# Two window-attention blocks on one core: a new order on the step grid, X loaded image by image, constant rows written by ScalarE

## The chip, the cores and the metric

The kernel runs on one core of a Trainium2 chip. The metric is the device time of one execution in microseconds (us), lower is better; 2% is about what the runs of this kernel can tell from no change. TensorE, VectorE (DVE), ScalarE (ACT), GpSimd (POOL) and SyncE (SP) each work through their own list of instructions in order and wait on semaphores.

## The reference

Two transformer blocks in a row, each on 8 images of 16x16 tokens with 192 channels, in fp32:

```
xn   = layer_norm(x) * w + b
win  = 14x14 windows of xn padded to 28x28          # 4 windows an image, 196 tokens each
q,k,v = win @ qkv_w + qkv_b                         # 12 heads of 16
attn = softmax(q*scale @ k.T + rel_h(q) + rel_w(q)) # over all 196 keys, padded ones too
x    = x + (attn @ v) @ proj_w + proj_b
x    = x + gelu(layer_norm(x)*w+b @ fc1_w + fc1_b) @ fc2_w + fc2_b
```

The second block has its own weights and a different epsilon.

## The kernel before

The 8 images go through layer 0 and then through layer 1, as a pipeline of 16 "images" n = 0 to 15 (layer L = n // 8). X stays in SBUF for all images. An image's tokens are ordered so that the first 224 are the window's columns and the last 32 the edge.

For one image the steps are: the statistics and the normalised `xhat` of the first norm (`stats1`, GpSimd's `root1`, `hat1`), transposes and a split in a high and a low fp32r part (`norm1`, `low1`), the products `q`, `k`, `v`, the relative-position products `rel0` and `rel1` (28 small matmul rows each) and their transposes `rel_tok`. All of these use one PSUM bank, `front`. GpSimd makes the low parts of q, k and rel; SP copies them row group by row group into `q_stack` and `k_stack` (`qk0`, `rel0`, `stack1`: 20 DMAs an image), so that one product of 108 rows gives a head's scores. Then come, for each of 12 heads, `by_query` (scores with the queries in partitions) and `row_max`; `top` joins the maxima; `neg_top` transposes them and SP adds them as two rows to `q_stack`; `by_key` gives the scores again, transposed and with the maximum taken off, and ScalarE's `probs` exponentiates them. `times_v` (three groups of four heads), `to_tokens`, `att`, `proj`, the second norm (`stats2`, `root2`, `hat2`, `norm2`, `low2`), `fc1` (three pairs), ScalarE's `gelu` and `fc2` end the image. The padded keys are worked out apart, on GpSimd and VectorE (`pad_...`). ScalarE changes its function table between exponentials and gelus.

The order on each engine is written out by hand as a grid. Each engine has a table of ticks (`PE_AT`, `ACT_AT`, `DVE_AT`, `POOL_AT`, `SP_AT`), and `run` emits a step of image n at tick 48 n + its own:

```python
for now in range(min(ticks), PERIOD * (2 * IMAGES - 1) + max(ticks) + 1):
    for step in steps:
        for n in range(2 * IMAGES):
            if now - PERIOD * n in ticks:
                step(n, n // IMAGES, n % 2, now - PERIOD * n)
```

So ticks give an order and no time. The steps of up to four images stand between each other. The bank `back1` (`BB[1]`) is shared by `neg_top`, `proj` and two pairs of fc1; `issued` and `neg_tops_out` write the waits that follow from the order.

All loads stand in SP's one list. In the kernel before it begins with image 0's X, `ident`, vectors, qkv weights and masks; then the constant rows of both stacks (a mask and one-hot rows, rounded by GpSimd's `round_rows` to `rows_rounded` and copied 12 times by four DMAs); between them the rest of X in one DMA; then projection and fc2 weights and biases of both layers, then fc1's weights of layer 0 (`load_w1`) into the buffer that qkv's weights leave, and only then the grid, with `qk0` of image 0 first. The weights are split in high and low parts by ScalarE and VectorE (`weights1`, `weights2`), and norm biases go through the weights as small products (`bias0`, `bias1` for qkv, `bias2` for fc1).

## Time and profile before

| | us |
|---|---|
| runs (3) | 671.58, 660.64, 670.36; median 670.36 |
| the profiled execution | 666.7 |
| its span, first to last instruction | 664.8 |
| TensorE busy | 558.1 (84%) |
| VectorE, ScalarE, GpSimd busy | 361.0, 305.5, 236.1 |
| mean granted TensorE clock | 0.902 |

Times in rows are us from the span's start. "[x <-A]" behind a row is the engine's idle time before it and what ended it. A granted clock of 1.00 is 2.4 GHz and 0.50 is 1.2 GHz; the records begin some 80 us into the span, and before that the rows' own durations tell the level. A busy TensorE isn't TensorE at its peak.

### The profile page before, as it was taken

Reading aid. Unit: us, or ns where it says so; the run is one execution under the profiler, and the core shown is the slowest. Engines: PE = TensorE matmul, PEld = TensorE weight load, DVE = VectorE, ACT = ScalarE, POOL = GpSimd, SP = SyncE. Lnnn points to the kernel's source line nnn. Section 1 sums busy time; section 2 is a strip of 40 time slices with the busy share of each in tenths; the row PEclk is TensorE's granted clock in tenths of the full one; section 3 lists DMA queues with packets and bytes.
Section 4 is the critical chain, followed back from the end, with each engine's and each line's share of the span. In section 5 each row is a group of like instructions: output and inputs, shape, how many; then the busy total and the mean of one; then the engine's idle time right before and its main releaser. Section 6 shows DMA issues by size and latency. Waiting matters only on the chain.

```text
span 664.8 us, 12602 instructions
## 1 busy us (share of the span) xinstructions
PE 558.1 (84%) x4440; PEld 502.5 (76%) x4440; DVE 361.0 (54%) x914; ACT 305.5 (46%) x614; POOL 236.1 (36%) x424
## 2 busy tenths in 40 slices
PE   5700778989898989899998989898989998978766
PEld 4700667779797979798897978797979887967646
DVE  3210265685848484856448575758584767473221
ACT  1100113347463736464344737474745574746522
POOL 2001354253625343441515252354444263430100
PEclk9999977599989898997689988999897999999777
DMA  4416523322222222224112222222231323220000
GB/s 99 107 47 172 107 52 70 85 68 69 52 54 58 58 59 58 59 58 101 42 37 45 61 55 58 59 57 61 57 72 43 86 53 76 57 71 27 1 12 13
DMA packets 45674, 41.10 MB, mean 62 GB/s; under 512 B 6268, under 2 KB 44588, under 8 KB 45612
## 3 DMA queue, kind: packets, MB, share of 16 engines
q1 hardware_dynamic: 45612, 40.29, 25.9%
q8 instruction: 36, 0.59, 0.4%
q14 instruction: 26, 0.21, 0.1%
HBM read 6.80 MB, written 1.57 MB: 13 GB/s over the span
## 4 chain that ended last, share of the span: by engine, by line
PE 55%; issue 13%; DVE 9%; SPq 9%; POOL 8%; ACT 3%; DMA 3%; POOLq 0%; DVEq 0%; ACTq 0%
PE front L917 11%; PE back L831 10%; PE back L1073 9%; PE by_key L940 5%; PE by_query L971 5%; PE front L831 4%; DVE xhat L671 3%; SPq L297 3%; PE times_v L957 2%; POOL norm_rstd L394 2%; SPq L293 2%; POOL pad_e L423 2%; SPq L289 2%; PE back L1053 1%; DVE att L750 1%
## 5 line engine op out<-in xcount | busy, mean ns | idle before, releaser
L768 DVE TENSOR_REDUCE row_max<-by_query 128x2 f32<-128x512 f32 x192 | 130.7, 682 | 48.9 <-PE by_query L971 47.7
L530 ACT ACTIVATE probs<-by_key 128x452 f32<-128x452 f32 x192 | 103.5, 543 | 84.9 <-PE by_key L940 84.3
L940 PE MATMUL by_key<-q_stack,k_stack 110*128 110x196 f32 (+1 forms) x384 | 89.7, 331 | 2.2 <-ACT probs L530 1.9
L971 PE MATMUL by_query<-k_stack,q_stack 108*128 108x256 f32 x384 | 84.8, 314 | 8.0 <-DMA q_stack<-rel_lo 7.7
L917 PEld LDWEIGHTS front<-q_grid,rel_heads 96*84 96x84 f32 x896 | 86.9, 181 | 3.8 <-ACT rel_t L556 1.9
L917 PE MATMUL front<-q_grid,rel_heads 96*84 96x32 f32 (+1 forms) x896 | 87.7, 265 | 2.2 <-ACT rel_t L556 1.4
L940 PEld LDWEIGHTS by_key<-q_stack,k_stack 110*128 110x128 f32 x384 | 63.9, 210 | 14.7 <-issue 7.3
L971 PEld LDWEIGHTS by_query<-k_stack,q_stack 108*128 108x128 f32 x384 | 65.5, 213 | 10.0 <-DMA q_stack<-rel_lo 9.5
L1073 PE MATMUL back<-w,hid 128*128 128x192 f32 x384 | 70.9, 337 | 0.4 <-ACT hid L595 0.3
L1073 PEld LDWEIGHTS back<-w,hid 128*128 128x128 f32 x384 | 65.0, 198 | 1.2 <-ACT hid L595 0.8
L831 PE MATMUL back<-xn_hi,w_hi 128*128 128x256 f32 x192 | 61.3, 328 | 2.7 <-DVE xn_hi L678 2.7
L831 PE MATMUL back<-xn_hi,w_lo 128*128 128x256 f32 x192 | 60.3, 323 | 0.0
L394 POOL TENSOR_TENSOR norm_rstd<-norm_var,minus_half 128x2 f32<-128x2 f32 x32 | 30.0, 939 | 75.4 <-DVE norm_var L663 74.1
L671 DVE TENSOR_TENSOR xhat<-xhat,norm_rstd 128x384 f32<-128x384 f32 x32 | 32.0, 1001 | 42.9 <-POOL norm_rstd L394 42.9
L715 DVE COPY rel_t<-front 84x448 f32<-84x448 f32 x16 | 9.9, 621 | 82.0 <-PE front L917 82.0
L448 POOL TENSOR_TENSOR pad_w<-pad_w,pad_prod 128x36 f32<-128x36 f32 x16 | 4.2, 263 | 138.5 <-ACT pad_w L570 138.5
L831 PEld LDWEIGHTS back<-xn_hi,w_hi 128*128 128x128 f32 x192 | 45.7, 238 | 3.6 <-DVE xn_hi L678 3.6
L957 PE MATMUL times_v<-probs,v_ones 128*32 128x256 f32 (+1 forms) x768 | 48.2, 370 | 0.0
L831 PEld LDWEIGHTS back<-xn_hi,w_lo 128*128 128x128 f32 x192 | 45.2, 236 | 0.0
L488 POOL CAST rel_hi<-rel_t 84x512 fp32r<-84x512 f32 x32 | 19.5, 609 | 71.9 <-DVE rel_t L716 59.0
L595 ACT ACTIVATE hid<-back,b_real 128x256 f32<-128x256 f32 x96 | 38.8, 473 | 10.6 <-PE back L831 10.4
L490 POOL TENSOR_TENSOR rel_lo<-rel_t,rel_hi 84x512 fp32r<-84x512 f32 x32 | 40.8, 1276 | 2.6
(142 smaller groups left out, 1102.7 us busy)
## 6 DMA issues: line engine op xcount, KB each, us to landing
q_stack<-q_hi SPq DMA_DIRECT2D x64, 96.0 KB
k_stack<-k_hi SPq DMA_DIRECT2D x64, 96.0 KB
q_stack<-rel_hi SPq DMA_DIRECT2D x64, 84.0 KB
q_stack<-rel_lo SPq DMA_DIRECT2D x64, 84.0 KB
q_stack<-q_lo SPq DMA_DIRECT2D x32, 96.0 KB
k_stack<-k_lo SPq DMA_DIRECT2D x32, 96.0 KB
out<-X SPq DMA_DIRECT2D x8, 192.0 KB, 2.2
k_stack<-xn_hi SPq DMA_DIRECT2D x2, 744.0 KB
```

Of the source, the lines that this page charges most:

```text
L394: pool.tensor_tensor(norm_rstd[i][:, :], norm_var[i][:, :], minus_half[:, :], ALU.pow).then_inc(n_rstd[i], 1)
L490: pool.tensor_tensor(rel_lo[par][:, w, :, :], rel_t[:, w, :, :], rel_hi[par][:, w, :, :].bitcast(F32), ALU.subtract).then_inc(s_rlo, 1)
L530: act.activation(probs[h % NP][:, :], KB[h % 2][:, 0:KEYS], ACT.Exp).then_inc(s_ex, 1)
L595: act.activation(hid[:, m, :], fc1_psum(m), ACT.Gelu, bias=b1_real[L][:, m:m + 1]).then_inc(s_ge, 1)
L671: dve.tensor_tensor(xhat[i][:, :, :], xhat[i][:, :, :], norm_rstd[i][:, :].unsqueeze(2).broadcast_to([P, TILES, D]), ALU.mult).then_inc(n_ ...
L768: dve.tensor_reduce(row_max[:, h, :], QB[h % 2][:, :].rearrange("p (a t) -> p a t", a=TILES), AX, ALU.max).then_inc(s_smax, 1)
L831: last = pe.matmul(psum, lhs, rhs, start=(i == 0), stop=(i == len(chunks) - 1))
L917: last = pe.matmul(dst[:, :, at, :], rel_heads[L][:, w, WS - 1 - i:2 * WS - 1 - i, :] .rearrange("p k h -> p (k h)"), grid[:, :, at, :], s ...
L940: last = pe.matmul(KB[h % 2][:, lo:hi], k_stack[par][0:ROWS, h, c * P:(c + 1) * P], q_stack[par][0:ROWS, h, 0:hi - lo], start=True, stop=True)
L957: last = pe.matmul(VB[i * VW:(i + 1) * VW, 0:hi - lo], v_ones[n % NV][:, c, h, :], probs[h % NP][:, lo:hi], start=(c == 1), stop=(c == 0))
L971: last = pe.matmul(QB[h % 2][:, a * TOK:(a + 1) * TOK], q_stack[par][0:R_MAX, h, a * P:(a + 1) * P], k_stack[par][0:R_MAX, h, :], start=Tr ...
L1073: last = pe.matmul(BB[0][:, a * D:(a + 1) * D], hid[:, m, a * P:(a + 1) * P], w2[L][:, m, :], start=(m == 0), stop=(m == MC - 1))
```

## The change

- X is loaded image by image, each into its own semaphore, in SP's grid (`x` at the very start).
- The constant rows of both stacks are written by ScalarE (`stack_constants`: four copies of a whole stack from `key_rows` and `query_rows`), two at the start of its list and two after image 0's `q_grid`. GpSimd's `round_rows` and the four DMAs go, and so do the waits of `norm2` and `by_query` for them; SP's first `qk0` of each stack waits instead.
- The late weights of a layer (`load_late`) are asked for in SP's grid, layer 0's after image 1's stacks and layer 1's after image 3's; `proj_b` of layer 0 comes earlier. Each layer has its own semaphores. `load_w1` of layer 0 stands in the grid before image 0's `qk0`, qkv's weights of layer 1 one image later.
- fc1's bias product (`bias2`) is made before image 2's (10's) norm1 in place of image 1's (9's).
- Nearly all ticks of all five tables are new. On TensorE image 0's list begins bias0, norm1, q, k, v, rel0, rel1, rel_tok, then norm1, q, k, v of image 1, then by_query of image 0; before, bias2 and norm1 of image 1 and by_query of image 0 came ahead of q of image 1. On VectorE `setup` and `bias0` now come first. On ScalarE no `probs` stands between an image's three gelu steps. On GpSimd `fc2_bias` follows `root2` at once. The outputs are all stored after the last image's rows.

```diff
@@ -40,7 +40,7 @@
 V_LOADS = 16 * 2 * 2
-W_LOADS = 16 * 2 * 5
+W_LOADS = 16 * 3
 EPS = (1e-5, 1e-6)
...
@@ -48,20 +48,20 @@
 
-PE_AT = dict(bias0=-42, bias1=-51, bias2=-48, norm1=-47, q=-41, k=-35, v=-30, rel0=-21, rel1=-15, rel_tok=-11,
-             by_query=(5, 6, 10, 14, 18, 22, 25, 29, 31, 34, 39, 42), neg_top=52,
-             by_key=(56, 60, 62, 65, 72, 76, 77, 81, 83, 87, 92, 96), times_v=(74, 87, 104), to_tokens=106, att=110,
-             proj=114, norm2=123, fc1=(127, 128, 132), fc2=(140, 148))
-ACT_AT = dict(weights1=-45, weights2=40, norm1=-46, q_hi=-35, q_grid=-36, k_hi=-27, rel0=-14, rel_tok=-1, pad_e=26, pad_w=63,
-              att=116, neg_top=51, probs=(62, 64, 68, 74, 76, 78, 82, 86, 90, 95, 99, 103), norm2=124,
-              gelu=(132, 135, 137))
-DVE_AT = dict(stats1=-58, hat1=-52, low1=-47, weights1=-45, weights2=47, bias0=-43, bias1=-50, bias2=-49, setup=-31, q=-42, k=-32, v=-23,
-              rel1=-17, pad_max=15, pad_sum=27, pad_top=34,
-              row_max=(5, 9, 13, 15, 19, 25, 27, 28, 32, 37, 40, 43), top=45, times_v=(78, 88, 105), att=108,
-              x_att=116, stats2=120, hat2=120, low2=123, x_mlp=149)
-POOL_AT = dict(norm_b=-45, root1=-46, proj_bias=-32, pad_shift=23, pad_join=30, pad_arg=59, pad_mul=59, pad_sum=66,
-               pad_out=78, fc2_bias=128, root2=121, q_lo=-21, k_lo=-22, rel0=-6, rel1=-4)
-SP_AT = dict(qk0=-10, rel0=2, stack1=37, neg_top=66, wqkv=7, w1=-19, out=213)
+PE_AT = dict(bias0=-399, bias1=-54, bias2=-53, norm1=-47, q=-43, k=-42, v=-39, rel0=-30, rel1=-18, rel_tok=-11,
+             by_query=(17, 18, 24, 28, 29, 36, 37, 39, 40, 50, 51, 52), neg_top=54,
+             by_key=(57, 61, 62, 64, 68, 69, 73, 74, 79, 81, 85, 86), times_v=(72, 82, 102), to_tokens=109, att=119,
+             proj=121, norm2=131, fc1=(136, 144, 147), fc2=(149, 150))
+ACT_AT = dict(constants=(-384, -48), weights1=-79, weights2=39, norm1=-62, q_hi=-46, q_grid=-50, k_hi=-40, rel0=-30,
+              rel_tok=-20, pad_e=10, pad_w=67, att=107, neg_top=41,
+              probs=(46, 47, 53, 57, 58, 64, 66, 69, 70, 74, 85, 91), norm2=122, gelu=(126, 129, 132))
+DVE_AT = dict(stats1=-83, hat1=-70, low1=-45, weights1=-50, weights2=78, bias0=-338, bias1=-47, bias2=-51,
+              setup=-368, q=-36, k=-30, v=-22, rel1=-10, pad_max=23, pad_sum=27, pad_top=48,
+              row_max=(26, 28, 32, 35, 36, 38, 39, 48, 49, 50, 53, 55), top=55, times_v=(82, 92, 121), att=122,
+              x_att=129, stats2=130, hat2=130, low2=136, x_mlp=165)
+POOL_AT = dict(norm_b=-332, root1=-56, proj_bias=135, pad_shift=56, pad_join=67, pad_arg=77, pad_mul=115,
+               pad_sum=122, pad_out=137, fc2_bias=161, root2=161, q_lo=13, k_lo=13, rel0=21, rel1=27)
+SP_AT = dict(x=-803, late=-16, qk0=-96, rel0=-94, stack1=-72, neg_top=-45, wqkv=-97, w1=-98, out=348)
 
...
@@ -182,12 +181,13 @@
 
-        s_x0, s_x, s_const = sem("x0_loaded"), sem("x_loaded"), sem("const_loaded")
-        s_vec, s_w, s_wx, s_wy = sem("vectors_loaded"), sem("weights_loaded"), sem("wqkv_loaded"), sem("w1_loaded")
+        s_x, s_const = [sem(f"x{n}_loaded") for n in range(IMAGES)], sem("const_loaded")
+        s_vec, s_wx, s_wy = sem("vectors_loaded"), sem("wqkv_loaded"), sem("w1_loaded")
+        s_pb, s_b2, s_w = ([sem(f"{x}{L}_loaded") for L in range(2)] for x in ("proj_b", "fc2_b", "back_weights"))
         s_zero, s_wz = sem("buffers_zeroed"), sem("proj_weights_zeroed")
-        s_eps, s_rows, s_rounded = sem("eps_ready"), sem("stack_rows_loaded"), sem("stack_rows_rounded")
+        s_eps, s_rows = sem("eps_ready"), sem("stack_rows_loaded")
         s_id, s_col = sem("ident_loaded"), [sem(f"columns_loaded{L}") for L in range(2)]
-        s_setup, s_stack0 = sem("vectors_ready"), [sem(f"stack{i}_constants_loaded") for i in range(2)]
+        s_setup, s_stack0 = sem("vectors_ready"), sem("stack_constants_ready")
         s_nb, s_wxh, s_wxl = sem("norm_bias_widened"), sem("wqkv_hi_done"), sem("wqkv_lo_done")
...
@@ -270,39 +270,36 @@
 
-            sp.dma_start(x_slot(0, 0), x_t[:, 0:TILES, :]).then_inc(s_x0, 16)
-            sp.dma_start(ident[:, :], const["ident"]).then_inc(s_id, 16)
-            sp.dma_start(columns[0][:, :], layers[0]["columns"]).then_inc(s_col[0], 16)
-            load_wqkv(0)
-            sp.dma_start(columns[1][:, :], layers[1]["columns"]).then_inc(s_col[1], 16)
+            sp.dma_start(x_slot(0, 0), x_t[:, 0:TILES, :]).then_inc(s_x[0], 16)
             sp.dma_start(key_rows, const["key_rows"]).then_inc(s_rows, 16)
             sp.dma_start(query_rows, const["query_rows"]).then_inc(s_rows, 16)
+            sp.dma_start(columns[0][:, :], layers[0]["columns"]).then_inc(s_col[0], 16)
+            sp.dma_start(ident[:, :], const["ident"]).then_inc(s_id, 16)
+            load_wqkv(0)
+            sp.dma_start(pb[0][:, :], layers[0]["proj_b"].unsqueeze(0).broadcast_to([P, D])).then_inc(s_pb[0], 16)
             for name, tile in (("pad_mask", pad_mask[:, :, :]), ("head_mask", head_mask[:, :])):
                 sp.dma_start(tile, const[name]).then_inc(s_const, 16)
+            sp.dma_start(columns[1][:, :], layers[1]["columns"]).then_inc(s_col[1], 16)
             for L in range(2):
...
                 sp.dma_start(rel[L][:, :, :], p["rel"]).then_inc(s_vec, 16)
-            for par in range(2):
-                sp.wait_ge(s_rounded, 1)
-                for stack, lo, hi, c in ((q_stack, R_MASK, R_MAX, 1), (k_stack, R_RHI, ROWS, 0)):
-                    sp.dma_start(stack[par][lo:hi, :, :].bitcast(F32),
-                                 rows_rounded[lo:hi, c:c + 1, :].bitcast(F32).broadcast_to([hi - lo, HEADS, TOK])
-                                 ).then_inc(s_stack0[par], 16)
-                if par == 0:
-                    sp.dma_start(X[:, TILES:, :], x_t[:, TILES:, :]).then_inc(s_x, 16)
-            for L in range(2):
+
+            def load_late(L):
                 p = layers[L]
-                for tile, name in ((pb[L], "proj_b"), (b2[L], "fc2_b")):
-                    sp.dma_start(tile[:, :], p[name].unsqueeze(0).broadcast_to([P, D])).then_inc(s_w, 16)
+                if L == 1:
+                    sp.dma_start(pb[1][:, :], p["proj_b"].unsqueeze(0).broadcast_to([P, D])).then_inc(s_pb[1], 16)
+                sp.dma_start(b2[L][:, :], p["fc2_b"].unsqueeze(0).broadcast_to([P, D])).then_inc(s_b2[L], 16)
                 sp.wait_ge(s_wz, L + 1)
-                sp.dma_start(wp[L][:, 0, :], p["proj_w"][0:P, :]).then_inc(s_w, 16)
-                sp.dma_start(wp[L][0:LO, 1, :], p["proj_w"][P:D, :]).then_inc(s_w, 16)
-                sp.dma_start(w2[L][:, :, :], p["fc2_w"].rearrange("(m f) n -> f m n", f=P)).then_inc(s_w, 16)
-            sp.wait_ge(s_wxl, 1)
-            sp.wait_ge(s_wxh, 2)
-            sp.wait_ge(s_bx, 1)
-            load_w1(0)
+                sp.dma_start(wp[L][:, 0, :], p["proj_w"][0:P, :]).then_inc(s_w[L], 16)
+                sp.dma_start(wp[L][0:LO, 1, :], p["proj_w"][P:D, :]).then_inc(s_w[L], 16)
+                sp.dma_start(w2[L][:, :, :], p["fc2_w"].rearrange("(m f) n -> f m n", f=P)).then_inc(s_w[L], 16)
+
+            def setup(n, L, par, t):
+                if t == SP_AT["x"] and 1 <= n < IMAGES:
+                    sp.dma_start(x_slot(0, n), x_t[:, n * TILES:(n + 1) * TILES, :]).then_inc(s_x[n], 16)
+                if t == SP_AT["late"] and n in (0, 2):
+                    load_late(n // 2)
 
...
@@ -331,6 +328,8 @@
                 if t == SP_AT["qk0"]:
+                    if n < 2:
+                        sp.wait_ge(s_stack0, 2 * (n + 1))
                     load_qk_rows(n, par, 0)
...
@@ -346,22 +345,22 @@
             def store(n, L, par, t):
-                if t == SP_AT["wqkv"] and n == 2:
+                if t == SP_AT["wqkv"] and n == 3:
                     sp.wait_ge(s_wyl, 1)
...
                     load_wqkv(1)
-                if t == SP_AT["w1"] and n == IMAGES:
-                    sp.wait_ge(s_wxl, 2)
-                    sp.wait_ge(s_wxh, 4)
-                    sp.wait_ge(s_bx, 2)
-                    load_w1(1)
+                if t == SP_AT["w1"] and n % IMAGES == 0:
+                    sp.wait_ge(s_wxl, L + 1)
+                    sp.wait_ge(s_wxh, 2 * (L + 1))
+                    sp.wait_ge(s_bx, L + 1)
+                    load_w1(L)
                 if t == SP_AT["out"] and L == 1:
...
 
-            run(SP_AT, stack_neg_top, load_stacks, store)
+            run(SP_AT, setup, stack_neg_top, load_stacks, store)
             sp.wait_ge(s_out, 16 * IMAGES)
...
@@ -399,19 +394,16 @@
 
-            def widen_norm_b():
-                for L in range(2):
-                    pool.wait_ge(s_col[L], 16)
-                    pool.tensor_copy(norm_b[L][:, :, :],
-                                     n1[L][:, :, 1:2].broadcast_to([P, 2, P])).then_inc(s_nb, 1)
+            def widen_norm_b(L):
+                pool.wait_ge(s_col[L], 16)
+                pool.tensor_copy(norm_b[L][:, :, :], n1[L][:, :, 1:2].broadcast_to([P, 2, P])).then_inc(s_nb, 1)
 
             def biases_and_pads(n, L, par, t):
-                if t == POOL_AT["norm_b"] and n == 0:
-                    round_rows()
-                    widen_norm_b()
+                if t == POOL_AT["norm_b"] and n in (0, 1):
+                    widen_norm_b(n)
                 if t == POOL_AT["proj_bias"]:
                     pool.wait_ge(n_hat[0], n + 1)
-                    pool.wait_ge(s_w, W_LOADS)
+                    pool.wait_ge(s_pb[L], 16)
                     add_bias(L, n, pb[L], s_xb)
...
@@ -500,7 +493,15 @@
 
+            def stack_constants(par):
+                act.wait_ge(s_rows, 32)
+                for stack, rows in ((k_stack, key_rows), (q_stack, query_rows)):
+                    act.activation(stack[par][:, :, :], rows.unsqueeze(1).broadcast_to([P, HEADS, TOK]),
+                                   ACT.Copy).then_inc(s_stack0, 1)
+
             def weights(n, L, par, t):
+                if t in ACT_AT["constants"] and n == 0:
+                    stack_constants(ACT_AT["constants"].index(t))
                 if t == ACT_AT["weights1"] and n % IMAGES == 0:
...
@@ -515,9 +516,6 @@
                 act.wait_ge(s_vp if i == 0 else s_f1, n if i == 0 else MC * n)
-                if i == 1 and n == 0:
-                    for par in range(2):
-                        act.wait_ge(s_stack0[par], 32)
                 act.activation(xn_hi[i][:, 0, :], bank[:, 0:TOK], ACT.Copy)
...
@@ -618,7 +616,7 @@
                     scaled_lo(w1_lo, w1_in, n2[L], w1_hi, MLP, L, s_wyh, s_wyl)
-                if t == DVE_AT["bias2"] and n % IMAGES == 1:
+                if t == DVE_AT["bias2"] and n % IMAGES == 2:
                     dve.wait_ge(s_by, L + 1)
...
@@ -800,10 +798,8 @@
                 if t == DVE_AT["stats1"]:
-                    if n == 0:
-                        dve.wait_ge(s_x0, 16)
-                    else:
-                        dve.wait_ge(s_x, 16)
+                    if L == 0:
+                        dve.wait_ge(s_x[n], 16)
                     if L == 1:
...
@@ -963,8 +959,6 @@
                         pe.wait_ge(*stack_loaded(n, h // GH))
-                    if h == 0 and n < 2:
-                        pe.wait_ge(s_stack0[n], 32)
                     if HEADS * n + h >= 2:
...
@@ -1027,12 +1021,12 @@
                         pe.wait_ge(s_bxo, L + 1)
-                    if n % IMAGES == 1:
+                    if n % IMAGES == 2:
                         pe.wait_ge(s_byo, L + 1)
...
                     pe.wait_ge(s_ato, n + 1)
-                    pe.wait_ge(s_w, W_LOADS)
+                    pe.wait_ge(s_w[L], W_LOADS)
                     pe.wait_ge(s_zero, ZEROED)
```

## Rows read from the trace of the kernel before

**Rows 1.** The page, part 2: TensorE, busy tenths of the span in 40 slices.

```profile
PE   5700778989898989899998989898989998978766
```

**Rows 2.** Waits of TensorE, 0 to 99 us: line and releaser; us, times, longest.

```profile
PE front L844 <- DMA weights_in<-in_fc_w: 30.8, 1, 30.8
...
PE by_query L971 <- DMA q_stack<-rel_lo: 3.4, 1, 3.4
```

**Rows 3.** Timeline of SP's issues, 0 to 66 us: start, us, what.

```profile
10.15 14.94 SPq L293 DMA_DIRECT2D X<-in_x  x1
...
34.31 15.12 SPq L297 DMA_DIRECT2D pb<-in_proj_b  x1
```

**Rows 4.** Windows: length, each engine busy (instructions), granted clock, DMA share, GB/s.

```profile
159.84:578.43 418.59, 390.83 (x3308) 356.97 (x3307) 266.43 (x674) 228.13 (x460) 174.42 (x299) 0.92 0.26 59
194.50:229.14 34.64, 32.38 (x274) 29.82 (x273) 21.99 (x57) 18.77 (x39) 14.60 (x25) 0.90 0.26 56
295.42:338.15 42.73, 40.66 (x294) 36.61 (x293) 24.00 (x62) 20.12 (x41) 14.61 (x25) 0.80 0.28 64
515.60:547.18 31.58, 29.56 (x274) 26.78 (x273) 22.00 (x57) 18.79 (x39) 14.63 (x25) 1.00 0.30 68
603.57:664.80 61.23, 43.69 (x268) 37.17 (x266) 14.38 (x42) 23.48 (x42) 5.67 (x9) 0.77 0.04 14
```

**Rows 5.** Timeline of VectorE: the `top` of images 0 and 2.

```profile
99.03 0.18 DVE L792 TENSOR_TENSOR top<-row_max,pad_top 128x24 f32<-128x24 f32 x1
...
159.84 0.18 DVE L792 TENSOR_TENSOR top<-row_max,pad_top 128x24 f32<-128x24 f32 x1
```

**Rows 6.** Waits of TensorE, 515.6 to 547.18 us.

```profile
PE back L837 <- DVE xhat L671: 1.2, 1, 1.2
PE back L1053 <- DVE av_t L776: 0.3, 1, 0.3
PE by_query L971 <- DMA q_stack<-rel_lo: 0.3, 1, 0.3
```

**Rows 7.** Windows of 5 us beside the fall of the clock.

```profile
210.00:215.00 5.00, 3.24 (x41) 2.89 (x30) 4.49 (x8) 0.65 (x2) 4.90 (x11) 0.88 0.00 0
215.00:220.00 5.00, 5.00 (x26) 5.00 (x26) 1.02 (x2) 3.15 (x6) 3.10 (x4) 0.50 0.30 79
```

**Rows 8.** Timeline of all engines, 0 to 35 us: the front of image 0.

```profile
3.28 0.62 DVE L653 BATCH_NORM_STATS2 norm_s<-X 128x6 f32<-128x192 f32 x2 [3.28 <-DMA X<-in_x]
...
7.27 0.38 ACT L521 ACTIVATE xn_hi<-front 128x256 fp32r<-128x256 f32 x1 [5.18 <-PE front L839]
...
7.89 0.43 SPq L285 DMA_DIRECT2D att<-in_rel  x1
...
8.39 0.42 DVE L678 TENSOR_TENSOR xn_hi<-front,xn_hi 64x256 fp32r<-64x256 f32 x1
...
14.02 0.53 PE L831 MATMUL front<-xn_hi,wqkv_hi 128*96 128x256 f32 x1
...
21.27 0.49 DVE L644 TENSOR_TENSOR rel_heads<-att,head_mask 96x324 f32<-96x324 f32 x1
```

**Rows 9.** DMA issues of the whole run: queue, count, size, median us to landing.

```profile
att<-in_rel SPq DMA_DIRECT2D x2, 20.2 KB, 3.1
```

**Rows 10.** Groups by line and form, 121 to 590 us: busy us, mean ns, idle before.

```profile
L595 ACT ACT_TABLE_LOAD x26 | 33.4, 1283 | 0.5
...
L574 ACT ACTIVATE hid<-back 128x512 f32<-128x512 f32 x14 | 8.4, 598 | 23.4 <-PE back L1063 23.4
```

**Rows 11.** Timelines of VectorE and GpSimd, 520 to 552 us: second norm, `k_lo`, first norm.

```profile
528.73 0.56 DVE L814 TENSOR_TENSOR X<-X,back 128x384 f32<-128x384 f32 x1
...
531.49 1.61 DVE L671 TENSOR_TENSOR xhat<-xhat,norm_rstd 128x384 f32<-128x384 f32 x1 [0.59 <-POOL norm_rstd L394]
...
531.42 1.26 POOL L483 TENSOR_TENSOR k_lo<-k_t,k_hi 96x512 fp32r<-96x512 f32 x1
...
546.72 0.55 DVE L671 TENSOR_TENSOR xhat<-xhat,norm_rstd 128x384 f32<-128x384 f32 x1
```

7 lines of the change are left out of this document (2 added, 5 removed).

## The prediction, made before the changed kernel ran

> **What bounds the kernel now.** I read the page's slices first. TensorE is nearly full in the middle, and thin at both ends [rows 1]. TensorE's list of waits up to 99 us names the hole at the start: 30.8 us for fc1's weights, then 3.4 us for the last stack rows [rows 2]. The weights come late because SP's list stands in order behind 14.94 us of issuing the rest of X and 15.12 us of the next load [rows 3], with four copies of constant rows between. So one list of transfers sets the start.
>
> The stretches from one `top` to another come next [rows 4, 5]. From image 2's to image 14's are 418.6 us, 34.9 an image. One image at full clock took 31.58 us with TensorE busy for 29.56; the waits that ended there add up to 2.0 us (three are shown, the fourth is 0.2), 1.2 of them for the second norm's `hat2` [rows 4, 6]. TensorE is the bound with little idle, so a new order can take out at most these 2 us of a full-clock image. But the other image shown took 34.64 us with the same 274 matmul rows, at a granted clock of 0.90 [rows 4]. In detail: a stretch with 3.24 us of work in 5 is followed by five at 0.50, the 1.2 GHz level [rows 7]. So the hole costs twice where the clock falls: some 3.1 us more (34.64 - 31.58).
>
> **The start.** Five things change; the sum is for image 0's `top`, at 99.03 us now [rows 5].
> (a) The 30.8 us go: fc1's weights are asked for behind seven X loads and the first projection's end, and their bias product stands one image later, behind image 0's by_query steps. What is late next is the front chain of image 0. (b) The 3.4 us go: SP has nothing between image 0's rows and their wait. (c) Against it, VectorE's first step is now `setup`, which waits for the last small load. That load was issued at 7.89 us and is one place further back now; with the 3.1 us that its kind took to land it ends near 11.5. Two set-up pairs to 21.76 from 20.71 are 1.05 us (the last row of these shown), the bias sum 0.4. From the statistics' start (3.28) to `low1`'s end (8.81) are 5.5 us. So the first q product starts at 11.5 + 1.4 + 5.5 + 0.6 of hand-overs = 19.0, not 14.02: +5 us [rows 8, 9]. (d) ScalarE writes the constant rows: four copies of 128x3072. Nothing like it is in the trace; a 128x512 one took 0.598 [rows 10]. Bounds: 0.6 each if only the fixed part counted, 3.6 by length in proportion; I take 2.8, from the slope between 128x256 (0.38) and 128x512 [rows 8, 10]. The first two (5.6 us from about 4.6) end near 10.2, under the wait of (c), then the hi weights follow; the second two stand between `q_grid` and `q_hi`, where only SP's stack loads wait, and those are due 20 us later. Cost 0; if the cover failed, 0 to 7 us each pair. In return SP loses four copies of up to 744 KB. (e) q, k and v of image 1 now all stand ahead of image 0's first by_query: about +1 us net, as they were needed anyway.
> Sum: -30.8 - 3.4 + 5 + 1 = -28 us, `top` of image 0 at 71 (66 to 76).
> X in seven pieces costs seven issues of about 0.4 to 0.6 us in place of 14.94 [rows 3], beside VectorE's wait. The Trainium skill speaks against it ("DMA: Bandwidth & Descriptors", section Bandwidth: transfers should be batched to a MiB or more to get three quarters of the peak). By that rule the seven would take longer in total than the one of 1344 KB; the row shows the one held up by its queue for 14.94 us, and image 1 needs only its own piece, so the sum stays as it is.
>
> **The first two full images.** From image 0's `top` to image 2's are 60.8 us now [rows 5], much of it at the low level. The back half is not yet there, so they are bound by the chain, with fewer holes in the new order: I take 56, between 60.8 (nothing) and 50. That is -5.
>
> **The steady part.** I walked one image through the new order with starts and durations of the full-clock image. On TensorE it is now: norm1, two by_query, fc1's third pair, q, fc2, neg_top, k, fc2, times_v, v, two by_key, to_tokens, ..., att, by_query, times_v, proj, two by_key, two by_query, rel1, two by_key, times_v, norm2. Between proj's end and norm2 lie four score steps (0.24 us each), rel1 (2.2), two more and a times_v (0.9): 4.5 us. VectorE and GpSimd need 2.76 us from x_att's start to `hat2`'s (528.73 to 531.49) and then `hat2` itself: 3.4 us. It took 1.61 us beside GpSimd's `k_lo`, and 0.55 alone [rows 11]. In the new order GpSimd waits for `hat2` right after the root (`fc2_bias`), so nothing runs beside it. The 1.2 us wait goes, with 1.1 to spare; to_tokens and att also get 1 us and more of cover. What is late next is `low1` before q and `low2` before fc1, which come through ScalarE behind gelus: 0.2 to 0.4 us each. GpSimd's list (14.6 us busy an image [rows 4]) and SP's keep their cyclic order; neg_top's rows land 1.3 us before by_key asks.
> ScalarE's exponentials no longer stand between the gelus: two table loads of 1.283 us an image in place of four (two groups of 26 in 13 images, one of them shown [rows 10]). ScalarE isn't the bound, so 2.6 us saved count as cover only.
> So an image takes 29.6 + 0.6 = 30.2 us, bounds 29.6 and 31.6. Twelve are 362; the layer change adds bias products and weight splits, as now (42.73 us for the image with it [rows 4]): 9. That is 371 against 418.6: -47. It takes for granted that the clock stays at 2.4 GHz: no stretch as thin as the one before the fall is left, since both rel steps now stand among dense score steps.
> A rule against this is in the Trainium skill ("SBUF — State Buffer", Who interferes with whom: a VectorE instruction with both inputs in SBUF and a GpSimd one that reads SBUF shut each other out). The 1.61 beside 0.55 us agrees. By it `hat1`, which now falls beside `k_lo`, takes 1.1 us more; VectorE is busy 22 of 31.6 us there and `hat1` is due 10 us later, so it changes nothing unless VectorE becomes the bound.
>
> **The end.** The last `top` to the end are 61.2 us, TensorE busy 43.7 [rows 4]: a serial chain of the last two images. Its order is almost the same; fewer table loads give -1.5 (0 to -4).
> **Sum** for the profiled execution (666.7 us; span 664.8 and 1.9 around it): -28 - 5 - 47 - 1.5 = -81.5, so 585. The median of the runs is 670.4, so some 588; I say 587.
>
> **The rivals.**
> R1, the clock falls as often as now. For: it fell in the start inside rel steps with hardly a hole before them, and in the new order rel1, times_v and norm2 stand nearly together. Against: the clean falls follow the norm2 hole. Price 3.07 us (34.64 - 31.58) in some 9 of 12 images: +27, 613.
> R2, the steady part gains nothing, because a wait of the same size takes the place of `hat2`'s (my slacks are about 1 us, over 100 steps with four lists in order). Only the start is won: 670 - 34 = 636 (626 to 652).
> R3, the start isn't won, since `setup` and the constant rows hold the front longer: (d) uncovered for both pairs, +11, and the start's own slow clock, +3: 601. It lies in the range.
> R4, slower: TensorE stays at the low level through much of the steady part, because four mid-size waits keep it thin in place of one. An image of 29.6 us of work at half the granted rate costs up to 50. The start's gain of 34 over 14 images is 2.4 us each, so it decides from 34.9 + 2.4 = 37.3 us an image, a low share of over a third in place of 0.16 of the time (clock 0.92 [rows 4]). The start of before had such a share. It would give 690.
> That the change doesn't do what it says can't be: the loads are in the lists as written; R3 is what comes nearest.
>
> **How the numbers follow.** Forecast (570 to 602) 0.60; R1 0.17; R3 0.06; R2 0.12; R4 0.03; better than my bounds 0.02. The low end: start 66, images of 29.6, end -4, gives 566. Range 566 to 622: it leaves out R2, R4 and the tails, some 0.2. Within 2% (about what this kernel's runs can tell from none, 657 to 684) lies only the worst of R2: 0.03. Slower 0.03, faster 0.94.
>
> **What would show it.** First q product near 19 us; no wait over 7 us on TensorE after it; image 0's `top` near 71 and image 2's near 127; 30.2 us from one `top` to the next; the wait before norm2 gone; 2 table loads an image; a mean granted clock of 0.95 or more in the middle. The forecast is wrong if TensorE shows new waits of over 1 us in each image, above all before q, fc1's first pair or by_key, or if the clock falls in each image all the same.

## The result and the profile after

The changed kernel takes 570.7 us (median of four runs, 569.7 to 571.6). The kernel before took 668.2 us beside it (660.6 to 671.6). The ratio is 0.857, 95% interval 0.849 to 0.865. Some executions are in a slower state at a lower clock, and the ratios and their intervals leave those out (here the one of 671.6 us), while the medians don't, so the medians of the kernel before come out 2 to 5 us too high. The profiled execution's span is 568.8 us against 664.8.

The page's second part comes first again; it answers to [rows 1]. The second line is the granted clock of the same slices in tenths.

```profile
PE   3587989999999999999999999999999999989856
...
PEclk9999579999999999979998999999999999999987
```

TensorE is 90% busy or more from the seventh slice to the thirty-fifth. The clock falls at 59 us, in the slices with 243 and 308 us, and in the last images.

The windows of the changed kernel, cut at the `top` of images 2 and 14, 5 and 6, 6 and 7, and 15 and the end, answer to [rows 4]: length, then busy us of TensorE, its weight loads, VectorE, ScalarE and GpSimd, granted clock, DMA share, GB/s.

```profile
128.39:493.61 365.22, 362.84 (x3301) 330.66 (x3301) 271.23 (x671) 196.40 (x435) 170.38 (x299) 0.98 0.30 68
187.32:216.77 29.45, 29.25 (x274) 26.64 (x274) 22.51 (x56) 16.20 (x37) 14.20 (x25) 1.00 0.30 66
216.77:251.89 35.12, 34.92 (x293) 31.46 (x291) 24.81 (x60) 17.08 (x39) 15.13 (x25) 0.90 0.24 60
517.17:568.80 51.63, 37.43 (x262) 31.67 (x260) 14.00 (x42) 19.90 (x38) 7.65 (x12) 0.90 0.10 32
```

The twelve images of the first line took 418.59 us before, with TensorE busy for 390.83. So idle time went from 27.8 to 2.4 us (-25.4) and busy time from 390.8 to 362.8 us (-28.0) on nearly the same instructions (3308 and 3301). The second part is the clock: the same products at the high level are shorter. The gain in the middle is thus one half holes and one half clock.

The list of TensorE's waits in one steady image (187.32 to 216.77 us) has one row left. It answers to [rows 6], where three rows made up 1.8 us.

```profile
PE back L827 <- DVE xn_hi L676: 0.2, 1, 0.2
```

Where the 96.0 us of span went, between the `top` rows of VectorE at 77.97, 128.39, 493.61 and 517.17 us:

| stretch | before | after | forecast | measured |
|---|---|---|---|---|
| start to image 0's `top` | 99.0 | 78.0 | -28 | -21.1 |
| to image 2's `top` | 60.8 | 50.4 | -5 | -10.4 |
| to image 14's `top` | 418.6 | 365.2 | -47 | -53.4 |
| to image 15's `top` | 25.1 | 23.6 | (0) | -1.6 |
| to the end | 61.2 | 51.6 | -1.5 | -9.6 |

The start fell short, and these rows of its timeline say where; they answer to [rows 8]. The first is VectorE's `setup`, waiting for the last small load; the second is the first q product; the last three are image 1's second relative product, the first pair of fc1's bias product, and the transposes of the norm that come after it.

```profile
14.10 0.17 DVE L636 SCALAR_TENSOR_TENSOR kb_blocks<-head_mask,columns 96x12 f32<-96x12 f32 x1 [14.10 <-DMA att<-in_rel]
...
20.98 0.53 PE L827 MATMUL front<-xn_hi,wqkv_hi 128*96 128x256 f32 x1 [1.62 <-DVE xn_hi L676]
...
59.75 4.04 PE L913 MATMUL front<-q_grid,rel_heads 96*84 96x64 f32 x28
...
67.03 0.49 PE L840 MATMUL front<-columns,weights_in 128*128 128x1 f32 x2
...
73.61 0.66 PE L833 MATMUL front<-ident,xhat 128*128 128x128 f32 x2 [0.46 <-DVE b_real L621]
```

The q product stands at 20.98 and not at 19.0. The small load was issued at 8.36 us and landed 5.7 us later, not 3.1 [rows 9]; most of the delay has another cause, though, which the section on the prediction shows. And the relative product of 28 instructions takes 4.04 us, the time of the low level (2.2 at the high one), and fc1's bias product 6.1 us (67.03 to about 73.1). While it runs VectorE waits 7.43 us, and the last by_query steps of image 0 come behind it. So it lies on the path to image 0's `top`, as experiment 7 confirms.

### The profile page after: what moved, and what is told of

It is laid out like the page before. It is cut to its first block, busy times and chain, and to the rows that moved or that the text cites. A ratio compares the mean times of both kernels' runs of the same rounds, so it can differ in the third digit from the quotient of the medians.

```text
span 568.8 us, 12594 instructions
## 1 busy us (share of the span) xinstructions
PE 522.0 (92%) x4440; PEld 468.5 (82%) x4440; DVE 367.0 (65%) x914; ACT 277.3 (49%) x588; POOL 230.9 (41%) x423
## 4 chain that ended last, share of the span: by engine, by line
PE 68%; issue 14%; DVE 8%; POOL 5%; SPq 1%; ACT 1%; DMA 1%; DVEq 0%; POOLq 0%; ACTq 0%
PE back L827 12%; PE front L827 12%; PE front L913 11%; PE back L1067 9%; PE by_query L965 5%; PE times_v L953 5%; PE by_key L936 5%; DVE row_max L766 4%; DVE xn_hi L676 1%; POOL norm_rstd L389 1%; PE front L841 1%; PE front L840 1%; DMA att<-in_rel 1%; POOL X L394 1%; PE front L833 1%
## 5 line engine op out<-in xcount | busy, mean ns | idle before, releaser
L913 PE MATMUL front<-q_grid,rel_heads 96*84 96x32 f32 (+1 forms) x896 | 78.8, 252 | 1.4 <-ACT rel_t L554 0.7
L913 PEld LDWEIGHTS front<-q_grid,rel_heads 96*84 96x84 f32 x896 | 78.5, 166 | 1.9 <-DVE v_ones L703 0.9
L965 PE MATMUL by_query<-k_stack,q_stack 108*128 108x256 f32 x384 | 72.8, 305 | 1.6 <-DVE row_max L766 1.3
L936 PE MATMUL by_key<-q_stack,k_stack 110*128 110x196 f32 (+1 forms) x384 | 71.9, 304 | 2.2 <-DMA q_stack<-neg_top_t 1.1
L965 PEld LDWEIGHTS by_query<-k_stack,q_stack 108*128 108x128 f32 x384 | 56.6, 200 | 4.2 <-DVE row_max L766 3.3
L936 PEld LDWEIGHTS by_key<-q_stack,k_stack 110*128 110x128 f32 x384 | 53.3, 190 | 6.9 <-ACT probs L528 2.4
L827 PE MATMUL back<-xn_hi,w_lo 128*128 128x256 f32 x192 | 53.9, 293 | 0.0
L827 PE MATMUL front<-xn_hi,wqkv_hi 128*96 128x256 f32 x128 | 39.7, 320 | 6.5 <-DVE xn_hi L676 3.5
L827 PE MATMUL front<-xn_hi,wqkv_lo 128*96 128x256 f32 x128 | 37.1, 300 | 0.0
L953 PEld LDWEIGHTS times_v<-probs,v_ones 128*32 128x32 f32 x768 | 20.1, 109 | 17.8 <-issue 3.7
L472 POOL TENSOR_TENSOR q_lo<-q_t,q_hi 96x512 fp32r<-96x512 f32 x16 | 20.5, 1283 | 33.0 <-ACT q_hi L537 33.0
```

The costliest lines, as they stand in the source:

```text
L472: pool.tensor_tensor(q_lo[par][:, :, :], q_t[:, :, :], q_hi[par][:, :, :].bitcast(F32), ALU.subtract).then_inc(s_qlo, 1)
L827: last = pe.matmul(psum, lhs, rhs, start=(i == 0), stop=(i == len(chunks) - 1))
L913: last = pe.matmul(dst[:, :, at, :], rel_heads[L][:, w, WS - 1 - i:2 * WS - 1 - i, :] .rearrange("p k h -> p (k h)"), grid[:, :, at, :], s ...
L936: last = pe.matmul(KB[h % 2][:, lo:hi], k_stack[par][0:ROWS, h, c * P:(c + 1) * P], q_stack[par][0:ROWS, h, 0:hi - lo], start=True, stop=True)
L953: last = pe.matmul(VB[i * VW:(i + 1) * VW, 0:hi - lo], v_ones[n % NV][:, c, h, :], probs[h % NP][:, lo:hi], start=(c == 1), stop=(c == 0))
L965: last = pe.matmul(QB[h % 2][:, a * TOK:(a + 1) * TOK], q_stack[par][0:R_MAX, h, a * P:(a + 1) * P], k_stack[par][0:R_MAX, h, :], start=Tr ...
```

## The experiments

In each the theory called A is that of the prediction, or of my explanation of its miss. Unless another is named, each kernel is the changed one with the edit shown.

**1 and 2. The two parts apart.** The first has the new loads and constant rows with the old grid, the second the old loads with the new grid. The first cut is against the kernel before; ScalarE's table there also has the two steps of the constant rows, which the cut leaves out, and fc1's bias product is the late one.

```diff
 e1: PE_AT, ACT_AT, DVE_AT, POOL_AT as before
-SP_AT = dict(qk0=-10, rel0=2, stack1=37, neg_top=66, wqkv=7, w1=-19, out=213)
+SP_AT = dict(x=-803, late=-16, qk0=-96, rel0=-94, stack1=-72, neg_top=-45, wqkv=-97, w1=-98, out=348)
 e2: build() as before; all grids as after, without x, late and constants, and
+wqkv=-49
```

> The changed kernel's loads, constant rows and late bias product of fc1, in the grid of before (PE, ACT, DVE and POOL tables of before, with the two constant steps at the start of ScalarE's list and after q_grid). Theory A, start and order are two separate gains: the 30.8 us wait for fc1's weights and the 3.4 us for the stack rows go and nothing else, so 668 - 34 = 634 us (626 to 642), the wait of norm2 on hat2 stays at 1.2 to 1.8 us in each image, and the mean clock stays near 0.90. Rival B, the start is won only together with the order (another wait of the old grid ends late in its place): over 650. Rival C, the loads alone also mend the steady part: under 615.

> The loads, the rounded constant rows and the early bias product of before, in the new grid. Theory A: the hole of 30 us on TensorE before 66 us stays, images come every 29.5 us in the middle at full clock, and the end takes about 52 us in place of 61; the sum is the changed kernel's 571 plus 28 to 34, so 602 (595 to 610). Rival B, the order needs the new loads to run (SP's list blocks it later too): over 625. Rival C, the order is worth less than the trace of the changed kernel suggests, since the early start only moves the phase at which the clock falls: 620 to 635 with falls in most images.

Measured: the new loads alone 630.9 us, ratio 0.958 (0.947 to 0.969); the new grid alone 598.2 us, ratio 0.910 (0.904 to 0.916), against 662.1 for the kernel before on the same chip. In ratios that is 0.042 and 0.090 off, together 0.132, where both at once took off 0.143. Each of the three has an interval of about 0.01 to either side, so the parts add up as closely as these runs can tell. Both times lie where they were expected.

With the new loads alone image 0's `top` stands at 64.85 us, 34.2 sooner than before, the whole of terms (a) and (b) (in it 0.9 us are an earlier first q product, 13.07 for 14.02). With the new grid alone it stands at 105.28, 6.2 later, the size of (c) and (e) together, though other waits lie there as well. The middle remains as it was: the waits of TensorE between the `top` of images 2 and 14 still hold `hat2`'s, and the window is nearly that of before.

```profile
PE back L833 <- DVE xhat L669: 21.1, 12, 1.8
...
129.47:542.20 412.73, 384.02 (x3308) 351.40 (x3307) 266.41 (x674) 228.19 (x460) 174.09 (x299) 0.93 0.26 61
```

With the new grid alone the middle is that of the changed kernel, and a little better:

```profile
157.40:519.70 362.30, 359.99 (x3301) 328.22 (x3301) 271.24 (x670) 196.42 (x435) 170.02 (x299) 0.99 0.29 66
```

So the middle belongs to the grid and the start to the loads.

**3, 4 and 10. Give the hole back.** If the wait for `hat2` is what brought the clock down, putting the second norm's transposes six steps sooner, with all else left, should bring both back. The rival is that a hole costs only its own length. In the third kernel rel1 stands behind the hole; in the fourth it was to stand ahead of it; in the tenth it stands behind times_v.

```diff
-             proj=121, norm2=131
+             proj=121, norm2=125          # all three
-rel1=-18, rel_tok=-11
+rel1=-24, rel_tok=-11                     # the fourth
+rel1=-13, rel_tok=-9                      # the tenth, and VectorE's rel1=-9
```

> The changed kernel with TensorE's norm2 moved ahead of rel1, so that only four score steps lie between proj and norm2: a wait for hat2 of some 2.4 us in each image, straight before the rel products. Theory A, a hole ahead of rel products makes the clock fall: an image takes 29.5 + 2.4 at full clock and 3 us more where the clock falls, in most images, so 571 + 14 x 2.4 = 605 without falls and 625 to 640 with them; mean clock 0.93 or less. Rival B, the falls came from elsewhere (the phase, or the start): 605, clock 0.96.

> As the run before it, with rel1 moved ahead of proj, so that the same hole before norm2 is followed by by_key and times_v steps and not by rel products. Theory A, it is the hole and the thin rel products together that bring the clock down: the hole of 2 to 2.4 us stays, but few or no falls, 600 to 610 us, clock 0.95 or more. Rival B, the hole alone does it: the same time and clock as the run with the rel products behind it, within 1%.

> The transposes of the second norm stand 6 steps sooner on TensorE, and the second relative product and its copies behind times_v, so that by_key and times_v stand behind the hole instead of the relative products. Theory A (a short hole in each image costs mostly through the clock, wherever it stands): hat2's wait is 1.2 to 2.6 us an image, the clock falls in most images, an image costs 34 to 38 us instead of 29.46, and the total is 640 to 680. Theory B (only a hole that thin relative products follow brings the clock down): an image costs 29.46 plus the hole, 31 to 32 us, the clock stays above 0.95 and the total is 590 to 605.

Measured: 676.7, 715.3 and 668.6 us; the ratios are 1.029 (1.023 to 1.037), 1.090 (1.080 to 1.101) and 1.007 (1.002 to 1.013). One step moved by six places of the order undoes the whole gain of 14%. The first two expectations were well too low under every theory they named; the tenth kernel's theory A (640 to 680 us, a wait of 1.2 to 2.6 us, a fall in most images) came true. Waits and windows of TensorE from image 2's to image 14's `top`, of the third kernel:

```profile
PE back L833 <- DVE xhat L669: 30.7, 12, 2.8
...
137.70:596.00 458.30, 427.52 (x3301) 387.45 (x3301) 272.69 (x671) 195.32 (x435) 168.99 (x299) 0.82 0.24 55
```

and of the tenth:

```profile
PE back L833 <- DVE xhat L669: 30.8, 12, 2.8
...
140.60:584.60 444.00, 410.98 (x3301) 368.35 (x3301) 270.65 (x670) 194.93 (x435) 169.29 (x299) 0.87 0.24 56
```

The hole is 2.6 us an image in both (30.7 and 30.8 over 12). The third kernel's middle is 93.1 us longer than the changed kernel's, 28.4 of it idle (458.3 - 427.5 against 2.4) and 64.7 of it the same 3301 instructions at a lower clock. In the tenth it is 78.8 us, 30.6 idle and 48.1 clock. The fourth was no clean test: rel1 now comes so soon behind rel0 that it waits for ScalarE's copy of rel0's result out of the bank they share (`rel_t`, 18.4 us in 12 images), besides `hat2` (28.6 us). Its middle has 47.5 us idle and 443.8 busy, so it shows only that a second hole costs more of the same.

Three windows of the tenth kernel around one hole (197.59, 2.54 us of waiting) answer to [rows 7]:

```profile
190.00:195.00 5.00, 5.00 (x49) 4.21 (x47) 3.70 (x8) 2.75 (x8) 0.80 (x1) 1.00 0.35 96
195.00:200.00 5.00, 2.46 (x25) 1.55 (x24) 3.32 (x10) 1.99 (x6) 3.23 (x9) 0.84 0.24 41
200.00:205.00 5.00, 5.00 (x39) 4.61 (x32) 0.00 (x0) 0.00 (x0) 2.71 (x6) 0.50 0.00 0
```

The rival's condition, that only a hole with the relative products behind it brings the clock down, fell. In the tenth kernel transposes, two by_key and a times_v stand behind the hole, and the clock is at its low level in the window from 199 us, before the relative product begins:

```profile
198.00:199.00 1.00, 1.00 (x10) 0.71 (x12) 0.64 (x2) 0.51 (x2) 0.83 (x3) 0.70 0.00 0
199.00:200.00 1.00, 1.00 (x16) 0.40 (x8) 0.00 (x0) 1.00 (x4) 0.98 (x6) 0.50 0.00 0
...
200.40 4.13 PE L913 MATMUL front<-q_grid,rel_heads 96*84 96x64 f32 x28
```

In both kernels the clock falls beside each of the twelve holes. The falls last longer in the third, so the place has a share of it, 64.7 against 48.1 us.

**5 and 11. The exponential between the gelus.** In the changed kernel the twelve exponentials no longer part the three gelus. The fifth kernel puts the one of head 10 back, between the second gelu and the third, ahead of the copy of the next image's norm; the eleventh behind that copy.

```diff
-probs=(46, 47, 53, 57, 58, 64, 66, 69, 70, 74, 85, 91)
+probs=(46, 47, 53, 57, 58, 64, 66, 69, 70, 74, 82, 91)    # the fifth
+probs=(46, 47, 53, 57, 58, 64, 66, 69, 70, 74, 83, 91)    # the eleventh
```

> The softmax exponential of head 10 is put back between the first and the second gelu, so ScalarE changes its table four times an image instead of twice: two more loads of 1.28 us, and the second gelu ends about 3 us later. Theory A (the two fewer table loads are cover only, as the prediction had it): the second gelu is late for fc2 by 0 to 2 us; the steady images cost 29.5 to 31 us instead of 29.46, and the total is 571 to 592. Theory B (ScalarE's saving is a real part of the gain): the wait of fc2 on the second gelu is over 2 us in each image, the clock falls beside it as in the kernel before, and the total is above 600.

> The exponential of head 10 stands between the two gelus again, with its two table loads, but behind the copy of the next image's norm instead of ahead of it. Theory A (the run with the split ahead of that copy lost its 1.9 us an image because q waited for that copy; the table loads themselves are cover): q waits no longer, the second gelu ends 3 us later and fc2 waits 0 to 1 us, an image costs 29.5 to 30.5 us, and the total is 571 to 583. Theory B (two more table loads and the exponential cost an image about as much wherever they stand): fc2 waits for the second gelu by 1.5 to 3 us, an image costs 31 to 32.5 us, and the total is 590 to 610.

Measured: 600.3 us (597.8 to 604.0) and 579.1 us (577.9 to 581.2), ratios 0.911 (0.906 to 0.917) and 0.873 (0.869 to 0.877). The fifth's time lies at the edge of its theory B (over 600) and above A, but neither mechanism is the one that ran: fc2 doesn't wait for the gelus in the middle. The eleventh bears out its theory A. ScalarE's timeline of the fifth shows why:

```profile
189.28 1.28 ACT L528 ACT_TABLE_LOAD   x1
190.58 0.55 ACT L528 ACTIVATE probs<-by_key 128x452 f32<-128x452 f32 x1
191.02 0.38 ACT L519 ACTIVATE xn_hi<-front 128x256 fp32r<-128x256 f32 x1
...
191.67 1.28 ACT L593 ACT_TABLE_LOAD   x1
```

The copy of the next image's norm stands behind the table load and the exponential, VectorE's low part behind the copy, and q behind that. TensorE's wait for it is 19.0 us in eleven images, at most 1.9:

```profile
PE front L827 <- DVE xn_hi L676: 19.0, 11, 1.9
...
129.60:516.30 386.70, 365.49 (x3302) 333.31 (x3301) 271.35 (x672) 227.06 (x455) 170.41 (x299) 0.98 0.28 64
```

In the eleventh, q doesn't wait, and an ordinary image takes 29.8 us in place of 29.46. So two more table loads cost 0.35 us an image in the middle. In the last stretch they cost more: 57.0 us from image 15's `top` in the eleventh kernel, 60.8 in the fifth, 51.6 in the changed one, 61.2 before. fc2 waits there for the gelus:

```profile
PE back L1067 <- ACT hid L593: 3.4, 2, 2.1
```

The fifth kernel holds a second finding. Its hole before q, 1.7 us an image, is as long as the one that the kernel before had at the second norm in the same images:

```profile
PE back L837 <- DVE xhat L671: 19.1, 12, 1.8
```

Yet its middle has only 2.7 us more of busy time than the changed kernel's, where the kernel before had 28. The fifth kernel's window with one such hole (1.87 us) kept the full clock:

```profile
190.00:195.00 5.00, 3.13 (x25) 2.92 (x24) 3.14 (x9) 3.77 (x7) 0.84 (x2) 1.00 0.26 69
```

TensorE did less in these 5 us than in the stretch before the fall in [rows 7] (3.13 against 3.24). But the hole didn't leave the clock alone throughout. Of the nine holes of 1.9 us in the fifth kernel's middle, those that end at 159.7, 290.3 and 453.5 us are followed by a fall:

```profile
161.00:164.00 3.00, 3.00 (x12) 3.00 (x11) 2.77 (x11) 0.00 (x0) 1.67 (x3) 0.52 0.00 0
291.00:294.00 3.00, 3.00 (x13) 3.00 (x12) 2.71 (x10) 0.52 (x2) 1.22 (x2) 0.50 0.11 29
455.00:458.00 3.00, 3.00 (x11) 3.00 (x11) 2.61 (x10) 0.00 (x0) 1.87 (x3) 0.50 0.00 0
```

Each lasts 3.4 us. In the kernel before a fall of 3.4 to 10.2 us follows seven of the nine holes of 1.8 us in its middle. So a hole of nearly the same length brought the clock down in most images in one kernel and in a third of them in the other, and neither its length nor the busy share of 5 us tells by itself whether it will. What stands beside the hole differs: fc1 ahead and q and fc2 behind in the fifth, by_query and times_v ahead and the relative product behind in the kernel before. No run changed that alone with a hole of this length, so why the one costs more clock than the other stays open.

**6, 7 and 8. The start's two delays.** The sixth kernel takes VectorE's bias and setup out of the way of the first q product; the seventh moves fc1's bias product one image later; the eighth does both.

```diff
-bias0=-338, ... setup=-368
+bias0=-44, ... setup=-29                      # sixth, eighth
-if t == PE_AT["bias2"] and n % IMAGES == 2:   # and so on VectorE, and in norm1's wait
+if t == PE_AT["bias2"] and n % IMAGES == 3:   # seventh, eighth
-if t == SP_AT["wqkv"] and n == 3:
+if t == SP_AT["wqkv"] and n == 4:             # seventh, eighth
```

> VectorE's bias of q,k,v and its setup stand right ahead of the copy of q for image 0 and no longer ahead of the splits of the first weights. Theory A (the 2 us by which q.0 came later than forecast, 20.98 instead of 19.0, are the late landing of the small load, 5.7 us after its issue instead of 3.1): the first q product stands near 16 to 17, image 0's top near 73 to 74, and the time is 4 us less, 566 to 568. Theory B (the weight splits or the low parts of the image are as late anyway): q.0 stays at 20 to 21 and the time stays within 1 us of 570.7.

> The product of the second norm's bias through fc1 (12 pairs of narrow products) is moved one image later, and the next layer's q,k,v load with it. Theory A (it stood in image 0's path at the low clock, 6.1 us, and would take 3 us at the high one): image 0's top comes 6 us sooner, near 72, 3 us come back later, and the time is 3 us less, 567 to 569. Theory B (VectorE or the stack rows of image 0 hold its top anyway): image 0's top stays at 77 to 78 and the time stays within 1 us of 570.7, or rises by 3 us.

> The two edits before this one together. If both delays stand on the one chain to image 0's top, the gains add: 7 to 8 us, 562 to 565. If one hides the other, the total is that of the better of the two, 566 to 568.

Measured on one chip: 565.7 us (563.9 to 576.7), 569.2 (567.0 to 572.4) and 566.1 (562.8 to 572.1); ratios 0.859 (0.854 to 0.864), 0.864 (0.860 to 0.868), 0.858 (0.853 to 0.864). The first q product of the sixth comes at the expected place:

```profile
16.09 0.53 PE L827 MATMUL front<-xn_hi,wqkv_hi 128*96 128x256 f32 x1 [1.62 <-DVE xn_hi L676]
```

Image 0's `top` comes to 75.2 (73 to 74 expected), 72.7 and 68.5 us, from 78.0. So both delays lie on its path and they add (2.8 + 5.3 = 8.1, measured 9.5; the five other kernels with this start and X in seven pieces have that `top` at 77.3 to 79.3, so a difference of 1 us tells nothing). The total doesn't follow: the eighth is no faster than the sixth, where 562 to 565 were expected if the gains added. In the seventh, the step from image 0's `top` to image 1's takes 30.0 us in place of 23.0, and in the eighth 27.6: the bias product and the low clock went into the next stretch. Moving a step off one path put it on the next.

**9 and 12. X in one piece.** The ninth asks for the rest of X in one DMA, the twelfth does so with the sixth's late setup.

```diff
-if t == SP_AT["x"] and 1 <= n < IMAGES:
-    sp.dma_start(x_slot(0, n), x_t[:, n * TILES:(n + 1) * TILES, :]).then_inc(s_x[n], 16)
+if t == SP_AT["x"] and n == 1:
+    sp.dma_start(X[:, TILES:, :], x_t[:, TILES:, :]).then_inc(s_x[1], 16)
```

> The rest of X comes in one DMA instead of seven, asked for at the same place, and every image waits for it. Theory A (the seven requests and their descriptors right behind the small loads are what made the relative tables land 5.7 us after their issue instead of 3.1): the tables land 2 to 3 us sooner, the first q product stands near 18 to 19 instead of 21, and the time is 2 to 3 us less. Theory B (the landing is late for another reason, such as the queue's own load of small requests ahead of it): q.0 stays near 20 to 21 and the time stays within 1.5 us of 570.7; X lands before the first statistics of image 1 at 24 us either way.

> The late setup on VectorE together with X in one piece. With the setup late nothing waits for the small loads, so that one piece gains nothing more: 564 to 567, q.0 at 16. If image 1's part of X now lands later than its statistics want it (19.4 us), its norm and the product of q for image 1 come later by as much, and the time is 1 to 4 us above 565.7.

Measured on one chip: 572.5 us (569.6 to 575.2) and 568.5 us (567.2 to 570.2), ratios 0.863 (0.859 to 0.866) and 0.856 (0.853 to 0.859). In the ninth the single piece of 1344 KB lands 9.0 us after its issue (10.5 in the twelfth), and it is asked for once in 0.43 us instead of seven times in 3.72:

```profile
X<-in_x SPq DMA_DIRECT2D x1, 1344.0 KB, 9.0
```

The seven of 192 KB land after 5.9 us each, the last, issued at 12.1, near 18 us: about the time of the one (8.8 + 9.0, in the twelfth 8.8 + 10.5). The last small load lands 4.7 and 5.0 us after its issue with one piece, and 4.6 to 5.7 us in the ten kernels with seven, and the ninth's first q product stands at 20.09, so theory A of this experiment fell, and B has the place right. The edit between the ninth and the twelfth is VectorE's late setup and bias sum alone: 4.1 us, for the 4 that the sixth's expectation named (image 0's `top` comes 3.9 us sooner, 73.19 for 77.05).

The twelfth was expected at 564 to 567 and took 568.5. Image 1's part of X wasn't what held it: its `top` of image 2 comes at 125.27, 1.9 us before the sixth's 127.21. What it lost came later, through the clock: 365.2 us from there to image 14's `top` against 360.9, at a clock of 0.98 and 1.00.

The Trainium skill ("DMA: Bandwidth & Descriptors", section Bandwidth) wants transfers of a MiB or more. Here the batch neither gained nor lost what these runs can tell, and the whole of X landed within 2 us of the same time either way.

The fastest measured are the sixth and the eighth kernel, 565.7 and 566.1 us. Since the changed kernel's own 570.7 was taken on another occasion, and its ratio to the kernel before, 0.857, is the same as theirs, only the pair of the ninth and twelfth shows the gain of the late setup directly, and nothing shows a gain in the total from the later bias product.

## Why the prediction was right

The forecast was 587 us with a range of 566 to 622; measured are 570.7. The forecast mechanism is the one that ran; all four terms were mis-sized, three too small and one too large. In the total the start's miss of 7 us covers part of the other 21, so the sum came nearer than its terms did; that part is luck.

**The start, -28 forecast, -21.1 measured.** The loads' part, (a) and (b), was right to the microsecond: -34.2 in experiment 1. (c) was +5 and came out as +7: the q product at 20.98. The step that failed is the bias sum. I put it right behind the set-up pairs, at 12.6 us, as if its input were there. It waits for TensorE's bias products of q, k and v, and the sum has no such wait. Experiment 2 shows it: there the last small load landed in time (11.7 us for the 11.5 forecast), and the q product still came at 20.13.

```profile
11.74 0.17 DVE L638 SCALAR_TENSOR_TENSOR kb_blocks<-head_mask,columns 96x12 f32<-96x12 f32 x1 [11.74 <-DMA att<-in_rel]
...
14.23 0.16 DVE L629 TENSOR_TENSOR qkb_real<-times_v,columns 96x4 f32<-96x4 f32 x1 [1.43 <-PE times_v L855]
```

In the changed kernel these products end at 14.80 us and the bias sum starts at 15.08, so the late landing (5.7 us for 3.1) by itself cost about 0.3 us. The 3.1 was the median of two [rows 9], and the later of them had taken 3.5. It took 3.5 and 3.8 us in the two kernels that ask for the rest of X more than 2 us behind it, and 4.6 to 5.7 in the twelve that ask for X right behind it, in one piece or in seven. That X's bytes are the cause is likely, but no run leaves them out. (d) was right: the four copies took 2.76, 2.75, 2.75 and 2.75 us for 2.8 forecast, and nothing waits for them; here are two of them.

```profile
4.45 2.76 ACT L499 ACTIVATE k_stack<-hid 128x3072 fp32r<-128x3072 f32 x1 [2.42 <-DMA hid<-c_query_rows]
...
25.01 2.75 ACT L499 ACTIVATE k_stack<-hid 128x3072 fp32r<-128x3072 f32 x1
```

The other 5 us of the miss are a second step left out of the sum. I wrote that fc1's bias product stands "behind image 0's by_query steps". It stands behind most of them, but ahead of the last three, and it runs at the low clock. Experiment 7 gives its price on this path: 5.3 us, of which under 1 belongs to an earlier q product there.

**The first two full images, -5 forecast, -10.4 measured.** It is the lower bound of the term (50). The window of these two images has TensorE busy for 46.6 of 50.4 us at a clock of 0.98. I had kept a low clock for part of it, as before; it was over at 79 us.

**The middle, -47 forecast, -53.4 measured.** The wait for `hat2` is gone, and the spare time is as worked out: `hat2` takes 0.56 us, ends at 206.28, and the transposes start at 207.46, 1.18 us later for the 1.1 of the prediction.

```profile
205.72 0.56 DVE L669 TENSOR_TENSOR xhat<-xhat,norm_rstd 128x384 f32<-128x384 f32 x1 [0.25 <-POOL norm_rstd L389]
...
207.46 0.44 PE L833 MATMUL back<-ident,xhat 128*128 128x128 f32 x2
```

The Trainium skill's rule that VectorE and GpSimd shut each other out at the shared port ("SBUF — State Buffer", Who interferes with whom) agrees on both sides: nothing of GpSimd's runs beside this `hat2`. `hat1`, which now falls beside `k_lo`, takes 1.02 us, +0.5 and not the +1.1 that I allowed, and TensorE doesn't wait for it.

The new waits that I put at 0.6 us an image are 0.2: an image takes 29.46 us for the 30.2 forecast (TensorE's work in it is 29.25 us, for 29.6), twelve times 0.74, -9. Against it the layer's own products cost 11.7 us (365.2 - 12 x 29.46) for 9 forecast. They hold two of the falls of the clock: in the `top` step from image 5 to 6 (35.12 us) and from 7 to 8 (35.68 us), the first right behind and the second inside bias products with one column.

The two table loads less are cover in the middle, as I wrote, but only while the copy of the next norm stands ahead of them: 0.35 us an image in experiment 11, 1.9 in experiment 5.

**The end, -1.5 forecast, -9.6 measured.** TensorE's busy time fell from 43.7 to 37.4 us with the clock (0.77 to 0.90), and its idle time by 3.3. I sized the table loads by their length, as if TensorE kept its level. Experiments 5 and 11 show the term: with four loads an image the end is 57.0 to 60.8 us, at a clock of 0.85 and 0.77. In the ten kernels with two it is 51.6 to 53.9 us, so part of the changed kernel's 51.6 is luck. And of two waits each for `hat2` and `att` one each is left, as image 14's are covered now. The waits of TensorE from 603 us to the end, before:

```profile
PE back L837 <- DVE xhat L671: 6.1, 2, 3.5
PE back L1062 <- DVE att L756: 3.4, 2, 1.8
```

and from 517.17 us, after:

```profile
PE back L833 <- DVE xhat L669: 3.5, 1, 3.5
...
PE back L1056 <- DVE att L754: 1.8, 1, 1.8
```

No experiment took these waits alone.

**The rivals.** R1 had the clock fall as often as now. It fell in two of the twelve images, both at a layer's bias products. It had a real chance, though: experiment 3 is R1 and more, from one step six places away. R2, a wait of the same size in the place of `hat2`'s, is what experiment 5 built (1.9 us before q). It gave 600 and not 636, since that hole brought the clock down behind three of nine and for 3.4 us each. R3 held in part: `setup` and the bias sum did hold the front, by 4.1 us (experiments 9 and 12), but the constant rows didn't. R4 asked for 37.3 us an image; experiments 3 and 10 reach 38.2 and 37.0, with a clock of 0.82 and 0.87, and end at 677 and 669 us, so 1 to 3% slower. Its mechanism is real, and its point of decision lies where I put it, from one step's place.

## What to carry to other kernels

Where TensorE is the bound, read the idle time of a steady image and the granted clock as one number: compare an image at full clock with one at the low one, and price a hole that recurs in each image by both. Give such a step a spare microsecond rather than none, even where the hole is small; a hole that can't be avoided may cost less clock at another place (experiment 5), which only a run can tell. When a delay on the first image's path is taken away, follow the displaced work to its new place before you count the gain: experiments 7 and 8 brought image 0's `top` 5 and 9 us sooner, but their ratios to the kernel before (0.864 and 0.858) are no better than the changed kernel's 0.857. Before you call a load late, look at what else its reader waits for: with the load in time (experiment 2) the first q product was only 0.9 us sooner.
